# Token weights brought by transfers, and GpSimd multiplying by them, in a fused attention and mixture-of-experts block

## The reference

```python
x = x + attention(layernorm(x), ctx, ctx, mask)
flat = layernorm(x)
logits = flat @ router_w.T
topk_scores, topk_idx = top_k(logits + router_bias, 2)
topk_scores = softmax(topk_scores)
combine = zeros((N, 16)).at[arange(N)[:, None], topk_idx].add(topk_scores)
hidden = silu(einsum('nd,kde->nke', flat, gate_proj)) * einsum('nd,kde->nke', flat, up_proj)
out = einsum('nk,nkd->nd', combine, einsum('nke,ked->nkd', hidden, down_proj))
x = x + out + (silu(flat @ sh_gate.T) * (flat @ sh_up.T)) @ sh_down.T
```

## Time and profile before

| | us |
|---|---|
| median of 3 runs (198.13 to 198.25) | 198.16 |
| the profiled execution | 197.66 |
| its span, first to last instruction | 195.9 |
| TensorE busy | 180.9 (92%) |
| VectorE busy | 164.2 (84%) |
| ScalarE busy | 128.2 (65%) |
| GpSimd busy | 90.5 (46%) |
| TensorE's granted clock, mean | 0.985 |

### The profile page before, as it was taken

How to read it: one execution, slowest core, us unless ns; L and a number is a source line. 1 busy time by engine, 2 the same in 40 slices (tenths; PEclk the granted TensorE clock), 3 DMA queues, 4 the chain that set the end, 5 groups by cost and what they waited for, 6 DMA issues and landing times.

```text
span 195.9 us, 4342 instructions
## 1 busy us (share of the span) xinstructions
PE 180.9 (92%) x1343; PEld 127.4 (65%) x1351; DVE 164.2 (84%) x510; ACT 128.2 (65%) x290; POOL 90.5 (46%) x152
## 2 busy tenths in 40 slices
PE   7689886989999999999979899999999999999973
PEld 7554644566666666666656577777777777777741
DVE  5487989998999999999997899778797798679881
ACT  3177893687899899999967755564445445555431
POOL 7059994099988888888767714300000000000000
PEclk9999998799999999999999999999999999999997
DMA  6899200000000000000000000000100010001001
GB/s 125 289 328 399 81 2 2 3 0 2 3 0 5 0 0 0 0 0 5 0 2 3 0 0 3 0 0 0 54 3 0 0 54 0 0 0 54 0 3 54
DMA packets 7008, 7.21 MB, mean 37 GB/s; under 512 B 848, under 2 KB 5456, under 8 KB 6864
## 3 DMA queue, kind: packets, MB, share of 16 engines
q1 hardware_dynamic: 5680, 5.56, 8.9%
q10 hardware_dynamic: 1312, 1.46, 2.6%
HBM read 5.97 MB, written 1.05 MB: 36 GB/s over the span
## 4 chain that ended last, share of the span: by engine, by line
PE 62%; DVE 22%; POOL 5%; DMA 3%; issue 3%; ACT 2%; ACTq 0%; DVEq 0%; POOLq 0%
PE bank L1095 37%; PE bank L1045 8%; DVE smax L834 4%; DVE prob L855 4%; PE bank L1027 3%; DMA mrow<-mask_row 3%; PE bank L1036 3%; PE bank L1135 3%; POOL k_blk L457 2%; PE bank L1016 2%; PE bank L1006 1%; DVE k_all L769 1%; DVE att L845 1%; DVE key_sum L760 1%; PE bank L1001 1%
## 5 line engine op out<-in xcount | busy, mean ns | idle before, releaser
L649 ACT ACTIVATE sig<-bank 128x512 f32<-128x512 f32 x36 | 21.4, 598 | 33.7 <-PE bank L1095 33.4
L1045 PE MATMUL bank<-k_blk,q_blk 128*128 128x512 f32 x64 | 34.3, 620 | 0.4 <-issue 0.2
L457 POOL TENSOR_TENSOR k_blk<-k_all,consts_sb 128x512 f32<-128x512 f32 x32 | 33.1, 1056 | 0.0
L894 DVE TENSOR_TENSOR hid_u<-sig,bank 128x512 f32<-128x512 f32 x32 | 21.9, 685 | 11.6 <-PE bank L1095 8.8
L1095 PE MATMUL bank<-xt_hi,w_hi 128*128 (+1 forms) x72 | 29.3, 407 | 0.1
L1095 PE MATMUL bank<-xt_lo,w_hi 128*128 (+1 forms) x72 | 28.1, 390 | 0.0
L1095 PE MATMUL bank<-xt_hi,w_lo 128*128 (+1 forms) x72 | 28.1, 390 | 0.0
L903 DVE TENSOR_TENSOR hid_lo<-hid,hid_hi 128x512 fp32r<-128x512 f32 (+1 forms) x37 | 25.2, 682 | 0.7 <-ACT hid_hi L658 0.5
L602 ACT ACTIVATE prob<-prob,exp_scale 128x512 f32<-128x512 f32 x32 | 23.8, 744 | 1.8 <-DVE prob L855 1.8
L658 ACT CAST hid_hi<-hid 128x512 fp32r<-128x512 f32 (+1 forms) x37 | 22.2, 602 | 2.5 <-DVE hid L910 2.3
L834 DVE TENSOR_REDUCE smax<-bank 128x8 f32<-128x512 f32 x32 | 21.9, 683 | 2.0 <-PE bank L1045 2.0
(11 more groups left out here) (126 smaller groups left out, 353.5 us busy)
## 6 DMA issues: line engine op xcount, KB each, us to landing
w_moe_sb<-w_moe SPq DMA_DIRECT2D x1, 1296.0 KB, 9.0
xt_sb<-x_t ACTq DMA_DIRECT2D x4, 256.0 KB, 7.9
ctxt_sb<-ctx_t SPq DMA_DIRECT2D x4, 256.0 KB, 8.7
x_sb<-x SPq DMA_DIRECT2D x4, 256.0 KB, 10.7
out<-x_sb SPq DMA_DIRECT2D x3, 256.0 KB, 2.3
w_moe_sb<-w_moe SPq DMA_DIRECT2D x1, 432.0 KB, 8.0
w_att_sb<-w_att SPq DMA_DIRECT2D x1, 264.0 KB, 4.6
sel_sb<-expert_sel SPq DMA_DIRECT2D x1, 256.0 KB, 8.4
```

The source lines that it names most:

```text
L457: last = nc.gpsimd.tensor_tensor(k_blk[p][:, g, :, :], k_all[:, bass.ds(t, 1), g, :].broadcast_to([P, HG, S]), hmask_sb.rearrange("p (h o) ...
L649: nc.scalar.activation(sig[r][:, :], gate_ps[r][:, :], ACT.Silu).then_inc(s_sig, 1)
L894: nc.vector.tensor_tensor(dst[:, :], sig[r][:, :], up_ps[r][:, :], ALU.mult).then_inc(s_hid_u, 1)
L1045: nc.tensor.matmul(score_ps[g][:, :], q_blk[q][:, g, :, :].rearrange("p b s -> p (b s)"), k_blk[q][:, g, :, :].rearrange("p h s -> p (h s) ...
```

## The change

The weights no longer go through TensorE and PSUM. `comb` and `comb_b` are now one tensor for each half, with the experts ahead of the tiles, so that one f32 transpose (`weights_as_rows`, one matmul) gives 128 rows of 128 tokens (16 experts times 8 tiles). ScalarE copies it to `comb_row`, SP stores it to a buffer in the chip's DRAM (`weights_out`, and waits until it has landed), and then loads for every pair of a group two rows of 512 weights, each spread over 64 partitions, into one of four buffers `cb` (`weights_of_pair`). `in_parts`, `comb3`, `comb_t`, its clearing by GpSimd, the selection matrix and `token_weights` are gone, with their two constant inputs. `weighted` reads `cb` from SBUF instead of a bank. VectorE does it for units 1 to 5 of group 0; from unit 6 of group 0 on GpSimd does it.

The wait for `hid` of the unit two before, which keeps `hid_u` from being overwritten, moves from TensorE's up to VectorE's product. Beside these, four things move. The first transfer of the row mask is issued ahead of that of the activations. `keys` and `norm1` of groups 2 and 3 are done in steps 0 to 3, one of the four in each (before: both in step 0, both in step 1), and `rstd1_of` follows in steps 0, 2 and 3. `weights_of_two` of the first half goes from step 13 to step 12 and `combined` from step 14 to step 13. The first half's transpose stands in step 15 behind the gate of unit 0.

```diff
+CB_BUFS = 4
+            def weights_out(half):
+                sp.wait_ge(s_ct_sb, half + 1)
+                sp.dma_start(comb_dram[half].rearrange("e (t n) -> (e t) n", n=P), comb_row[half][:, :])\
+                    .then_inc(s_comb_out[half], 16)
+                sp.wait_ge(s_comb_out[half], 16)
+            def weights_of_pair(g, pair):
+                n = g * EPAIRS + pair
+                if n >= CB_BUFS:
+                    sp.wait_ge(s_hid, n - CB_BUFS + 1)
+                cols = slice(g % 2 * GN, (g % 2 + 1) * GN)
+                for e in range(2):
+                    sp.dma_start(cb[n % CB_BUFS][e * E_DIM:(e + 1) * E_DIM, :],
+                                 comb_dram[g // 2, 2 * pair + e:2 * pair + e + 1, cols].broadcast_to([E_DIM, GN]))\
+                        .then_inc(s_cb[n % CB_BUFS], 16)
+            for g in range(GROUPS):
+                if g % 2 == 0:
+                    weights_out(g // 2)
+                for pair in range(EPAIRS):
+                    weights_of_pair(g, pair)
+                    if pair == EPAIRS - 2 and g > 0:
+                        result_out(g - 1)
...
+        def weighted(eng, ops, g, m):
+            n, r, k = g * UNITS + m, m % 2, (m - 1) % CB_BUFS
+            eng.wait_ge(s_hid_u, n + 1)
+            eng.wait_ge(s_cb[k], 32 * (g * (EPAIRS // CB_BUFS) + (m - 1) // CB_BUFS + 1))
+            if exists(g, m, back=3):
+                eng.wait_ge(s_hid_lo, n - 2)
+            ops.tensor_tensor(hid[m % 3][:, :], hid_u[r][:, :], cb[k][:, :], ALU.mult).then_inc(s_hid, 1)
...
-            expert_weights(pool, nc.gpsimd, 1, s_route[1])
+            combined(pool, nc.gpsimd, 1, s_route[1])
+            for m in range(6, UNITS):
+                weighted(pool, nc.gpsimd, 0, m)
+            with pool.Fori(0, GROUPS - 1) as i:
+                for m in range(1, UNITS):
+                    weighted(pool, nc.gpsimd, i + 1, m)
...
             act.dma_start(mcol8[:, :], mask_col).then_inc(s_mask_col, 16)
+            act.dma_start(mrow8[:, 0:GN], mask_row[:, 0:GN].broadcast_to([P, GN])).then_inc(s_mask_row[0], 16)
             act.dma_start(xt_sb[:, 0:GN], x_t[:, 0:GN]).then_inc(s_xtin[0], 16)
-            act.dma_start(mrow8[:, 0:GN], mask_row[:, 0:GN].broadcast_to([P, GN])).then_inc(s_mask_row[0], 16)
...
-                if isinstance(t, int) and 0 <= t < GROUPS - 2:
-                    keys(t + 2)
-                    norm1(t + 2, t % 2)
+                if isinstance(t, int) and 0 <= t <= TRAIL:
+                    g = 2 + t // 2
+                    if t % 2 == 0:
+                        keys(g)
+                    else:
+                        norm1(g, g % 2)
                 if isinstance(t, int) and t == TILES - 4:
                     experts_marked(0)
+                    weights_of_two(0)
                 if isinstance(t, int) and t == TILES - 3:
-                    weights_of_two(0)
-                if isinstance(t, int) and t == TILES - 2:
                     combined(dve, nc.vector, 0, s_route[0])
-                if isinstance(t, int) and t == TILES - 1:
-                    in_parts(dve, nc.vector, 0, s_route[0], range(PARTS))
...
+                if m >= 3:
+                    dve.wait_ge(s_hid, g * EPAIRS + m - 2)
+                elif m > 0 and not isinstance(g, int):
+                    dve.wait_ge(s_hid, g * EPAIRS + m - 2)
...
-            def weights_as_rows(half, bank):
-
-                pe.wait_ge(s_comb3, half + 1)
-                for k in range(2 * GT):
-                    last = nc.tensor.transpose(bank_bf16(bank)[0:PARTS * EXPERTS, k * P:(k + 1) * P],
-                                               comb3[:, k, :, :].rearrange("p k e -> p (k e)"), identb_sb[:, :])
-                last.then_inc(s_ct, 1)
+            def weights_as_rows(half):
+
+                pe.wait_ge(s_route[half], 2)
+                nc.tensor.transpose(ct_ps, comb[half][:, :, :].rearrange("p e t -> p (e t)"), ident_sb).then_inc(s_ct, 1)
...
-            def token_weights(g, m):
-                pe.wait_ge(s_ct_sb, min(m, 2) if isinstance(g, int) else 4)
-                nc.tensor.matmul(cb_ps[m % 2][:, :], sel_sb[:, m - 1, :], comb_t[:, bass.ds(g * GN, GN)], start=True,
-                                 stop=True).then_inc(s_cb, 1)
```

129 lines of the change are left out of this document (43 added, 86 removed).

## The result

The changed kernel takes **201.67 us** (median of four runs, 200.86 to 203.69) against 198.14 (197.83 to 198.25) for the kernel before in the same comparison: ratio 1.0196, 95% interval 1.0115 to 1.0277. It is slower by 3.5 us; I had forecast 196.9, faster by 1.3. A run more than 1.5% above the fastest of its kernel counts as slow and is left out of the ratios in this document; there is one (201.35 us, before_with_spread).

A forecast was written before the change was run, and what follows sets the result against it. TensorE, busy throughout both long stages, was taken as the bound. Profiled 197.66 + 1.1 (expert stage) - 1.3 (end of attention) - 0.45 (mask row) - 0.6 (spread) = 196.4, plus 0.5 to the median: 196.9 us, range 193.0 to 202.0.

The forecast's parts named there:

- Sharing between GpSimd and VectorE, group +0.62: Expert loop: weightings and low parts wait for each other, so a group takes 21.5 us instead of 20.88.
- B: Expert loop: waits are full in most units, groups of 22.9 to 23.0 us, kernel at 202; chance 0.20.
- C: Expert loop: requests fall in gaps with little waiting, groups of 19.0 us, kernel at 189.5; chance 0.10.
- D: Weight transfers: the weights land late, so the change fails its purpose, kernel at 198 to 204; chance 0.07.
- Group 0, -1.34 forecast: First low part to copy of group 0's sum: -1.83 + 0.8 - 0.45, and +0.14 for two slots of group 1.
- eight matmuls less, -1.83: Group 0: TensorE loses eight token-weight matmuls, saving 1.83 us.
- the seven transposes (-0.45): Second half's weights: eight transposes become one, saving 0.45 us.
- units 6 to 8 behind the routing steps: Group 0: unit 6's weighting queues on GpSimd behind three routing steps; with the first hole +0.8 us (0 to 1.7).
- End of attention, -1.3 forecast: VectorE's five weight-splitting steps go, so the residual sum begins at 102.51 instead of 103.75: -1.3 us (-0.5 to -2.9).
- Start, mask row -0.45: Start: the first mask row, which VectorE waits for, is issued before the activations, saving 0.45 us (0 to 0.5).
- Start, spread -0.6: Start: keys and statistics of groups 2 and 3 spread over steps 0 to 3, saving 0.6 us (0 to 1.7).
- Last unit, +0.67: End of expert stage: nothing hides the last unit's slower GpSimd weighting, costing 0.67 us.

The follow-up runs named there:

- before_with_spread: The kernel before, with only the keys and norm-1 statistics of groups 2 and 3 spread over steps 0 to 3 and GpSimd's waits to match: 200.05 us.
- second profile: Profile of one further run of the unaltered changed kernel, at the full granted clock (1.000): 200.48 us, with a span of 198.7 us.
- low_from_psum: Changed kernel with keys and statistics placed as before; in groups 1 to 3 the low part subtracts an unused PSUM bank instead of the SBUF high part: 193.15 us.
- gpsimd_beside: weighting_on_vector plus, per unit of groups 1 to 3, a GpSimd multiplication of the same form on unneeded data that nothing waits for: 215.49 us.
- weighting_on_vector: Changed kernel with every multiplication by the token weights on VectorE, the weights still coming by the same transfers: 191.18 us, ratio 0.9648.
- units_678_on_gpsimd: norm_first with only the weighting of units 6 to 8 of group 0 back on GpSimd, behind the routing steps: 191.20 us.
- first profile: Profile of the slowest of the changed kernel's four runs, at a mean granted clock of 0.971: 203.69 us, with a span of 201.9 us.
- norm_first: weighting_on_vector with statistics before keys in the spread, and GpSimd's waits for the last keys moved to the end of its loop steps: 189.77 us.
- half_mask_first: norm_first with the half masks' two transfers issued ahead of the rest of the mask row: 191.22 us.

## Why the prediction was wrong, point by point

The forecast was 196.9 us and the median is 201.67, 4.8 more. Of that, 4.1 us stand in the table of stretches: 2.0 in group 0, 1.1 in the start, 0.7 in the two whole groups, 0.6 in the end of attention, and -0.3 in the last stretch. The other 0.7 is between single executions: the median lies 1.2 above the second profile's, and the forecast had added 0.5 for that.

- **Sharing between GpSimd and VectorE, group +0.62.** The mechanism was right: low parts of 1.35 to 1.57 us, weightings up to 1.72, products unharmed, TensorE idle before a down product. Shown by low_from_psum from one side and gpsimd_beside from the other. The term was small by a third of a microsecond a group: 21.83 instead of 21.5, +0.95, a loop of 7.28 us and not 7.18. The weighting by itself is 1.29 to 1.30 us, not 1.27. I had misread the row that I took as a confirmation: L481 in the earlier trace rows is nine subtractions, not three, and 1008 ns for 384 columns is 2.63 ns a column, against 2.46 for the 1258 of 512 columns; by it the weighting would have been 1.34. And sometimes the product waits too, up to 0.7 us, for the weighting two units earlier to have read its buffer: the wait that the change adds, which my loop had without a price.
- **Rivals.** B (full waits, 22.9) did not appear in any trace; C (19.0) is what the kernel gives as soon as the sharing is gone; D is out (the transfers land in 2.7 to 3.6 us, and neither engine waits for the weights).
- **Group 0, -1.34 forecast, +0.65 measured: the largest miss, 2.0 us.** Two steps of it failed. First, "eight matmuls less, -1.83" and the seven transposes (-0.45) were booked whole. With all weightings on VectorE the stretch from the first low part to the copy is 130.22 - 110.11 = 20.11 us against 21.23 before, so -1.1 for both. TensorE's own work fell nearly as booked, from 20.94 to 19.00 us, but of its saving 0.8 us turned into idle time (1.11 of the 20.11 us, where it had been 0.29 of 21.23): it waits 0.97 and 0.26 us for two low parts. VectorE was nearly as full as TensorE there, in the kernel before already, since it still does the last attention tiles. Its stages of the kernel before, and under them those of weighting_on_vector (columns as in the earlier trace rows; VectorE is the third busy time):

```profile
112.00:116.00 4.00, 4.00 (x20) 2.96 (x19) 3.67 (x14) 2.71 (x7) 1.39 (x2) 1.00 0.00 0
116.00:120.00 4.00, 4.00 (x19) 2.98 (x18) 3.83 (x11) 2.10 (x4) 0.00 (x0) 1.00 0.00 0
120.00:124.00 4.00, 4.00 (x18) 3.05 (x18) 3.86 (x7) 1.74 (x4) 3.48 (x8) 1.00 0.02 4
```

```profile
112.00:116.00 4.00, 3.98 (x19) 2.75 (x18) 3.82 (x5) 2.60 (x7) 2.73 (x3) 1.00 0.22 80
116.00:120.00 4.00, 3.74 (x16) 2.71 (x17) 3.75 (x14) 2.05 (x4) 0.00 (x0) 1.00 0.32 117
120.00:124.00 4.00, 4.00 (x18) 2.96 (x17) 4.00 (x10) 2.36 (x4) 2.21 (x3) 1.00 0.37 131
```

  That VectorE's fullness is what makes these low parts late is my reading of the shares; no run took work off it to show it. Second, units 6 to 8 behind the routing steps: 0.8 forecast, 130.47 - 108.59 = 21.88 against 20.11, that is 1.8 in the traces of the changed kernel and weighting_on_vector, and 1.4 to 1.6 in the medians of units_678_on_gpsimd.
- **End of attention, -1.3 forecast, -0.7 measured.** The residual sum that began at 103.75 begins at 102.51, behind the output projection, as forecast. What I didn't ask is what is late next. Changed kernel, second profile:

```profile
102.51 0.29 DVE L809 TENSOR_TENSOR x_sb<-x_sb,bank 128x128 f32<-128x128 f32 x1 [1.56 <-PE bank L1012]
...
103.61 1.28 ACT L665 ACT_TABLE_LOAD   x1
...
105.65 0.47 PE L1104 MATMUL bank<-xt_hi,w_hi 128*128 128x512 f32 x1 [0.17 <-ACT sig L665]
```

  ScalarE loads its table for Silu at 103.61 for 1.28 us in both kernels, at the same time, and TensorE's next gate waits for the Silu behind it. Of the 1.24 us only 0.62 was left at the first low part.

  That 102.51 came exactly has some luck in it. I had put the move of `weights_of_two` and `combined` to earlier steps at 0. It makes the first score difference of tile 15 late by 1.22 us (96.85 instead of 95.63), though that of tile 12 was 0.07 late; before_with_spread, without the move, has no such delay (4.78 and 4.53 us from tile 13 to 14 and from 14 to 15, as in the kernel before; 5.35 and 5.11 now). TensorE begins the gate of unit 0 at 99.06 instead of 97.84 and then works without a pause from 98 to 104 us (6.00 of 6, 5.01 before), so the projection ends where it did before. Whether it would have come earlier without the move no run shows.
- **Start, mask row -0.45: nothing left of it.** The first row did land earlier (the share row begins at 6.77 instead of 8.18), but in ten of the eleven profiles the keys of group 0 then wait for the half masks, which land at 11.5 to 12.5. The first score difference of the kernel lies at 17.8 to 19.0 us in the eleven profiles with the new order of issue, 18.5 in the mean, and at 18.50 and 18.25 in the two with the old one. I read the wait of 1.99 us and didn't look at the transfer behind it.
- **Start, spread -0.6: wrong in sign.** It gained 2.5 us up to step 2 (the score difference of tile 3 at 37.19 instead of 39.73, second profile), gave 1.5 back in steps 2 and 3, where the work now is, as I had said, and the other 1.1 in step 4 (5.59 us from score difference to score difference and not 4.53; 7.43 in the first profile, when the clock fell). The failed step is "GpSimd ... gets one rstd later", costed at nothing: I took the moved instruction for its own length and didn't ask whose result it waits for at the new place, and what stands behind it on GpSimd.
- **Last unit, +0.67.** From the last copy to the end it is +0.87 where +1.15 was forecast. At the measured pace of a group the seven slots alone are +0.74, which leaves 0.1 for this term. TensorE had holes before the last units already, 0.53 and 0.59 us in the kernel before; now it is one of 2.1.
- **The clock.** I named a fall in the expert stage as what would make the prediction wrong. It came, but in the first half, and at the very end. Between the run at the full clock (200.48) and the median (201.67) lie 1.2 us, between it and the first profile 3.2.
- **The chances.** 0.35 for slower held the outcome, and the range up to 202.0 held the median, but not for its reason (groups of 23): that it was held is luck.

The version that the experiments led to, norm_first (weights by transfers, every weighting on VectorE, statistics before keys), takes 189.77 us, 4.2% less than the kernel before. So one part of the change, taking the token weights off TensorE by transfers, is worth more than the whole forecast (weighting_on_vector, 191.18 us, is 6.9 under the kernel before); the other, moving the multiplication to an idle engine, costs 8.7 us.

## What to carry to other kernels

An idle GpSimd is not free beside a full VectorE: before moving an elementwise operation there, count the VectorE operations with two SBUF inputs beside it, and try the version that leaves it where it is. When a matmul or a step is taken out, ask in that very stage which second engine is as full, and what is late next; whole-stage shares of the settled loop don't hold for the stage where two phases overlap. When an instruction is moved on an in-order queue, price the wait for its input at the new place and everything queued behind it, not its length.

## What the runs showed that I had not expected

- An operation on GpSimd that nobody waits for (two SBUF inputs, 128x512, 1.29 us alone) cost 1.0 us of the kernel's time each, 24.3 us for 24, when VectorE was full with operations of two SBUF inputs.
- The same hole in TensorE's work, 1.4 to 1.5 us idle in a stage of 4, was followed by a granted clock of 0.53 for 5 us in one execution and by 1.00 in another of the same kernel. A fall there cost 2.8 us; so a kernel with such holes can scatter more: 2.8 us over four runs, against 0.55 in norm_first and 0.4 in the kernel before beside it (which in its other comparisons scattered by 0.7 to 0.8 over seven runs and 1.4 over seventeen).
- Two transfers of 64 KB issued ahead of another of 192 KB (half_mask_first) made that one land at 11.41 us, and the kernel 1.4 us slower; half of the delay came only because a key mean then fell beside a GpSimd operation (0.84 us instead of 0.17).
- 32 token-weight matmuls replaced by 64 transfers of 128 KB were worth 1.6 us a group (20.88 to 19.27), and no engine waited for these transfers.
